# Second cross attention: a row of its own for the queries' bias in the score product

## The reference

```python
def _L1_xattn_ref(q, k, v, Wq, bq, Wk, bk, Wv, bv, Wo, bo):   # 16 heads of 8
    qh = (q @ Wq + bq).reshape(B, LQ, HEADS, D_K).transpose(0, 2, 1, 3)
    kh = (k @ Wk + bk).reshape(B, LKV, HEADS, D_K).transpose(0, 2, 1, 3)
    vh = (v @ Wv + bv).reshape(B, LKV, HEADS, D_K).transpose(0, 2, 1, 3)
    scores = jnp.einsum('bhqd,bhkd->bhqk', qh, kh) * (1.0 / np.sqrt(D_K))
    attn = jax.nn.softmax(scores, axis=-1)
    out = jnp.einsum('bhqk,bhkd->bhqd', attn, vh)
    return out.transpose(0, 2, 1, 3).reshape(B, LQ, D_MODEL) @ Wo + bo

x = _layernorm(x + _L1_xattn_ref(x, ctx_512, ctx_512, ...), axis=-1)
```

## Time and profile before

| | |
|---|---|
| median of 3 runs | 689.21 us (686.73 to 691.59) |
| profiled execution | 686.46 us |
| its span, first to last instruction | 684.7 us |
| mean granted TensorE clock | 0.999 |
| PE busy | 634.4 us (93%) |
| DVE busy | 507.3 us (74%) |
| ACT busy | 335.1 us (49%) |
| POOL busy | 348.3 us (51%) |
| chain that ended last | PE 72%, DVE 13%, ACT 9%, issue 5% |

### The profile page before, as it was taken

One profiled execution on the slowest core, in us unless ns is written; L12 is line 12 of the kernel. 1 busy time (PEld: TensorE's weight loads), 2 busy tenths in 40 slices (PEclk: granted clock), 3 DMA queues, 4 the chain that ended last, 5 costly groups with the idle time before them and its releaser, 6 DMA issues.

```text
span 684.7 us, 20022 instructions
## 1 busy us (share of the span) xinstructions
PE 634.4 (93%) x8872; PEld 474.1 (69%) x8872; DVE 507.3 (74%) x822; ACT 335.1 (49%) x502; POOL 348.3 (51%) x257
## 2 busy tenths in 40 slices
PE   8798989999999999999898889899999999998997
PEld 4576766677777777777785656677776677776774
DVE  3666837799989888885464756798888988988443
ACT  2154463555646646635325244446556365464443
POOL 1362670188888888464110422195675755745400
PEclk9999999999999999999999999999999999999999
DMA  9600003000000000000040000000000000000000
GB/s 264 231 1 2 3 1 131 2 2 2 2 2 2 3 2 2 2 2 2 2 153 0 1 1 2 1 2 2 2 2 3 2 2 2 2 2 2 2 1 14
DMA packets 3506, 14.74 MB, mean 22 GB/s; under 512 B 372, under 2 KB 628, under 8 KB 3420
## 3 DMA queue, kind: packets, MB, share of 16 engines
q1 hardware_dynamic: 3420, 13.46, 5.9%
HBM read 13.23 MB, written 0.23 MB: 20 GB/s over the span
## 4 chain that ended last, share of the span: by engine, by line
PE 72%; DVE 13%; ACT 9%; issue 5%; DMA 1%; DVEq 0%; ACTq 0%
PE psum L987 18%; PE psum L891 10%; PE psum L200 6%; PE psum L940 5%; PE psum L933 5%; PE psum L935 5%; DVE scratch L1085 2%; DVE scratch L1070 2%; PE psum L870 2%; ACT scratch L1054 2%; PE psum L897 1%; PE psum L224 1%; PE psum L879 1%; PE psum L229 1%; PE psum L909 1%
## 5 line engine op out<-in xcount | busy, mean ns | idle before, releaser
L1070 POOL TENSOR_TENSOR scratch<-scratch 125x896 bf16<-125x896 f32 x136 | 234.9, 1734 | 173.1 <-ACT scratch L1054 173.0
L1054 ACT ACTIVATE scratch<-psum 125x896 f32<-125x896 f32 x192 | 173.8, 917 | 175.6 <-PE psum L987 173.8
L1085 DVE TENSOR_REDUCE scratch<-psum 128x1 f32<-128x500 f32 x336 | 210.7, 673 | 16.6 <-PE psum L891 8.1
L987 PE MATMUL psum<-scratch 128*125 128x448 bf16 (+1 forms) x768 | 177.2, 355 | 9.1 <-issue 8.8
L891 PE MATMUL psum<-scratch 128*128 128x500 bf16 x336 | 126.0, 375 | 2.0 <-ACT nrm L1021 0.8
L987 PEld LDWEIGHTS psum<-scratch 128*125 128x125 bf16 (+1 forms) x768 | 97.3, 136 | 39.8 <-issue 9.5
L933 PE MATMUL psum<-tok,scratch 125*128 125x65 bf16 x1344 | 108.9, 195 | 1.8 <-DVE kT L1130 1.8
L935 PE MATMUL psum<-tok,scratch 125*128 125x64 bf16 x1344 | 108.3, 192 | 0.0
L933 PEld LDWEIGHTS psum<-tok,scratch 125*128 125x128 bf16 x1344 | 95.5, 97 | 13.8 <-issue 2.6
L935 PEld LDWEIGHTS psum<-tok,scratch 125*128 125x128 bf16 x1344 | 90.3, 99 | 14.4
L200 PE MATMUL psum<-w_second 128*128 128x256 bf16 x638 | 85.3, 272 | 0.0
(11 more groups left out here) (311 smaller groups left out, 814.3 us busy)
## 6 DMA issues: line engine op xcount, KB each, us to landing
raw<-ctx_dram SPq DMA_DIRECT2D x4, 672.0 KB
w_third<-fifth_dram SPq DMA_DIRECT2D x3, 636.0 KB, 5.2
w_third<-third_dram SPq DMA_DIRECT2D x2, 844.0 KB, 21.2
w_third<-third_dram SPq DMA_DIRECT2D x2, 843.5 KB, 19.4
w_fourth<-fourth_dram SPq DMA_DIRECT2D x3, 542.5 KB, 6.1
w_first<-first_dram SPq DMA_DIRECT2D x1, 996.0 KB, 5.0
w_second<-second_dram SPq DMA_DIRECT2D x1, 834.0 KB, 6.9
w_third<-fifth_dram SPq DMA_DIRECT2D x1, 636.5 KB, 7.4
```

Source lines behind the costliest of these rows:

```text
L987: mm = nc.tensor.matmul(bank(S + f, HALF, CP), lhs[0:rows, CP * c:CP * c + CP], rhs[0:rows, HALF * f:HALF * f + HALF], start=(rows == 128) ...
L1054: nc.scalar.activation(CR["p"][0:CP, n % RING, :].rearrange("p (f n) -> p f n", f=2), psum[0:CP, S:S + 2, 0:HALF], ACT.Exp).then_inc(self. ...
L1070: ops.tensor_tensor(CR["pl"][0:CP, n % RING, :], CR["p"][0:CP, n % RING, :], p_high(n % RING), ALU.subtract).then_inc(done, 1)
L1085: nc.vector.tensor_reduce(mxp[:, r, t:t + 1], bank(B, TB), X_AXIS, ALU.max).then_inc(self.aux_freed, 1)
```

## The change

The low queries `qb` get the bias row as row 96, and `yb` has ones in the rows 64 to 96, so that the product adds it to every score. The rows between, 65 to 95 of `qb`, are zero. The second product of a score has 97 rows in the second attention where it had 65. ScalarE's copy goes to partition 96 of `qb`, not to partition 64 of `qx`, which is gone. In A, VectorE subtracts the bias row from the turned maximum and writes the result to row 64, once; the semaphore `top_set` and the addition behind it are gone. The ones rows cover 33 partitions in `cross2`, and GpSimd sets rows 64 to 95 of `qb` to zero in two more memsets before `cross2`; the first M of the batches 0 and 1 and, new, VectorE's A of the same batches wait for all of them.

```diff
--- before.py
+++ after.py
@@ -148,7 +148,6 @@
             CR["ya", i] = R.take([CTX], BF16)
             CR["yb", i] = R.take([CTX], BF16)
             CR["qa", i] = R.take([896], BF16)
-            CR["qx", i] = nrm[:, 7 * i:7 * i + 7, :].rearrange("p a b -> p (a b)").bitcast(BF16)
             CR["qb", i] = R.take([896], BF16)
         CR["p"] = R.take([RING, 896])
         CR["pl"] = R.take([RING, 896], BF16)
@@ -181,10 +180,14 @@
         tok_scaled = sem("token_scaled")
         y_ones = sem("y_ones")
 
-        def y_ones_set(pool, done):
+        def y_ones_set(pool, biased):
+
             for i in range(2):
-                nc.gpsimd.memset(CR["yb", i][64:65, :], 1.0).then_inc(y_ones, 1)
-                pool.wait_ge(y_ones, done + i + 1)
+                nc.gpsimd.memset(CR["yb", i][64:97 if biased else 65, :], 1.0).then_inc(y_ones, 1)
+                pool.wait_ge(y_ones, 2 * biased + i + 1)
+            for i in range(2 * biased):
+                nc.gpsimd.memset(CR["qb", i][64:96, :], 0.0).then_inc(y_ones, 1)
+                pool.wait_ge(y_ones, 5 + i)
 
         pads_set = sem("pads_set")
         key_scaled = sem("key_weights_scaled")
@@ -798,11 +801,11 @@
             def __init__(self, tag, src, wk, wv, biased):
                 self.tag, self.src, self.wk, self.wv, self.biased = tag, src, wk, wv, biased
                 (self.aux_ready, self.aux_freed, self.scores, self.probs, self.pv_done, self.mean_turned, self.tok_high,
-                 self.tok_set, self.ya_set, self.yb_set, self.q_high, self.max_set, self.top_set, self.rec_set, self.mean_set, self.low_dve,
+                 self.tok_set, self.ya_set, self.yb_set, self.q_high, self.max_set, self.rec_set, self.mean_set, self.low_dve,
                  self.low_pool, self.front_act, self.front_dve, self.front_low) = (
                     sem(f"{tag}_{n}") for n in (
                         "aux_ready", "aux_freed", "scores", "probs", "pv", "mean_turned", "tok_high", "tok_set",
-                        "ya_set", "yb_set", "q_high", "max_set", "top_set", "rec_set", "mean_set", "low_dve", "low_pool",
+                        "ya_set", "yb_set", "q_high", "max_set", "rec_set", "mean_set", "low_dve", "low_pool",
                         "front_act", "front_dve", "front_low"))
 
                 self.order = [(u, 0) for u in FRONT]
@@ -886,7 +889,7 @@
                         else:
                             pe.wait_ge(self.front_dve, 2)
                         if b < 2:
-                            pe.wait_ge(y_ones, 2 if self is cross1 else 4)
+                            pe.wait_ge(y_ones, 6 if self.biased else 2)
                     r, t = k // TBLK, k % TBLK
                     mm = nc.tensor.matmul(bank(B, TB), CR["qa", i][:, 128 * r:128 * r + 128],
                                           CR["ya", i][:, TB * t:TB * t + TB], start=True, stop=True)
@@ -982,11 +985,12 @@
                         pe.wait_ge(self.yb_set, 2 * (b + 1))
                         pe.wait_ge(self.front_low, 2)
                     S = 2 + 2 * (n % 2)
-                    for lhs, rhs, rows in ((CR["ya", i], CR["qa", i], 128), (CR["yb", i], CR["qb", i], 65)):
+                    below = 97 if self.biased else 65
+                    for lhs, rhs, rows in ((CR["ya", i], CR["qa", i], 128), (CR["yb", i], CR["qb", i], below)):
                         for f in range(2):
                             mm = nc.tensor.matmul(bank(S + f, HALF, CP), lhs[0:rows, CP * c:CP * c + CP],
                                                   rhs[0:rows, HALF * f:HALF * f + HALF],
-                                                  start=(rows == 128), stop=(rows == 65), skip_group_check=True)
+                                                  start=(rows == 128), stop=(rows != 128), skip_group_check=True)
                     mm.then_inc(self.scores, 1)
                     if c or not b:
                         sums_of_earlier()
@@ -1018,7 +1022,7 @@
                     nc.scalar.activation(CR["qa", i][0:64, cols], bank(B, HALF, 64), ACT.Copy)
                     ins = nc.scalar.activation(CR["qa", i][64:128, cols], bank(B, HALF, 64), ACT.Copy)
                     if self.biased:
-                        ins = nc.scalar.activation(CR["qx", i][64:65, cols], psum[64:65, B, 0:HALF], ACT.Copy)
+                        ins = nc.scalar.activation(CR["qb", i][96:97, cols], psum[64:65, B, 0:HALF], ACT.Copy)
                     ins.then_inc(self.q_high, 1)
                 elif kind == "T":
                     act.wait_ge(self.aux_ready, idx + 1)
@@ -1033,10 +1037,10 @@
                 act.wait_ge(self.aux_ready, 3)
                 nc.scalar.activation(CR["qa", 0][0:64, 0:HALF], bank(4, HALF, 64), ACT.Copy).then_inc(self.front_act, 1)
                 if self.biased:
-                    nc.scalar.activation(CR["qx", 0][64:65, 0:HALF], psum[64:65, 4, 0:HALF], ACT.Copy
+                    nc.scalar.activation(CR["qb", 0][96:97, 0:HALF], psum[64:65, 4, 0:HALF], ACT.Copy
                                          ).then_inc(self.front_act, 1)
                     act.wait_ge(self.front_dve, 1)
-                    nc.scalar.activation(CR["qx", 0][64:65, HALF:2 * HALF], psum[64:65, 5, 0:HALF], ACT.Copy
+                    nc.scalar.activation(CR["qb", 0][96:97, HALF:2 * HALF], psum[64:65, 5, 0:HALF], ACT.Copy
                                          ).then_inc(self.front_act, 1)
 
             def run_act(self, act):
@@ -1092,10 +1096,10 @@
                     lo, hi = (0, 512) if k == 0 else (512, 896)
                     shift, below = CR["qb", i][64:65, lo:hi], psum[64:65, B, 0:hi - lo]
                     if self.biased:
-                        bias = CR["qx", i][64:65, lo:hi]
-                        nc.vector.tensor_tensor(shift, below, bias, ALU.subtract).then_inc(self.top_set, 1)
-                        dve.wait_ge(self.top_set, 2 * b + k + 1)
-                        nc.vector.tensor_tensor(shift, shift, bias, ALU.add).then_inc(self.aux_freed, 1)
+                        if b < 2:
+                            dve.wait_ge(y_ones, 6)
+                        nc.vector.tensor_tensor(shift, below, CR["qb", i][96:97, lo:hi], ALU.subtract
+                                                ).then_inc(self.aux_freed, 1)
                     else:
                         nc.vector.tensor_copy(shift, below).then_inc(self.aux_freed, 1)
                 elif kind == "T":
@@ -1849,7 +1853,7 @@
                 cross1.split_tokens(pool, 0, k)
             pool.wait_ge(cross1.tok_set, 2)
             pool.wait_ge(a1_act.sem, a1_act.count(f"o{PAIRS-1}"))
-            y_ones_set(pool, 0)
+            y_ones_set(pool, False)
             for k in range(2):
                 cross1.split_tokens(pool, 1, k)
             cross1.run_pool(pool)
@@ -1867,7 +1871,7 @@
             cross2.split_tokens(pool, 1, 0)
             pool.wait_ge(ln_c.sem, ln_c.count("yr"))
             pool.wait_ge(cross2.tok_set, 3)
-            y_ones_set(pool, 2)
+            y_ones_set(pool, True)
             pool.wait_ge(outer, 4)
             cross2.split_tokens(pool, 1, 1)
             cross2.run_pool(pool)
```

## The result

The changed kernel takes 679.21 us (median of 4 runs, 677.76 to 681.06), the kernel before 690.3: a ratio of 0.9849 with a 95% interval of 0.9802 to 0.9896. Timed twice more, in other sets, the ratio was 0.9853 (0.9831 to 0.9876) and 0.9849 (0.9818 to 0.9880). The forecast was 679.0. The medians differ by 11.1 us in the first set and by 10.3 and 10.4 in the other two; 10.2 was forecast.

The account below looks back on a forecast made before the run. TensorE waits for VectorE's shift row at batch boundaries of the second cross attention. Savings of 8.4 + 0.64 + 0.84 + 0.3 = 10.2 us, against the median of 689.21, gave 679.0 us, range 675.0 to 683.5.

Parts of the forecast that it names:

- What bounds the boundary: Between batches of the second cross attention, TensorE's "issue" wait before a score product is for VectorE's shift row; 8.8 us over seven.
- Five boundaries at 1.68 us: Five batch boundaries of the second cross attention: score product starts at 461.33 instead of 463.01, together 8.4 us saved.
- The sixth and seventh, 0.64 and 0.84: Last two batch boundaries of the second cross attention, without GpSimd work beside them: 0.64 and 0.84 us saved.
- The front, 0.3: Before batch 0 of the second cross attention, where filler products cover most of the wait: 0.3 us saved.
- rival 1: Only TensorE's recorded idle time before score products goes: gain 9.1 us, time 680.1; chance 12%.
- Rival 3: New shift-row subtraction is slow, its second input lying in other partitions: gain 4.7 us, time 684.5; chance 7%.
- Rival 5: Another wait of the score product ends at the same moment, so nothing moves: 688 us; chance 3%.
- Rival 2: VectorE's next subtraction, started earlier, collides with GpSimd unabsorbed: 0.58 us at five boundaries, gain 7.3, time 681.9; chance 8%.
- the twin: First cross attention, same code without the keys' bias, read for comparison: 26.0 us a batch against the second's 27.8.
- The profiled execution: Whole kernel: 10.2 us off the profiled execution's 686.46 gives 676.3; against the median, 679.0.

## Why the prediction was right

- *What bounds the boundary.* Right: "issue" in front of the score product was VectorE's shift row. Taking the operation away alone empties the wait, the layout alone leaves it, and a second subtraction brings it back.
- *Five boundaries at 1.68 us.* The distance between the small reductions of two batches fell from 27.78 to 26.12 us, 1.66 each, 8.3 against 8.4.
- *The sixth and seventh, 0.64 and 0.84.* 26.76 to 26.13 is 0.63, and from the seventh boundary's reduction to the last chunk's score products 20.41 us (624.80 to 645.21) became 19.57 (618.77 to 638.34): 0.84.
- *The front, 0.3.* Mis-sized: 0.46. I took the row's idle time where I should have taken, as at the boundaries, the distance of the products in TensorE's queue. It is the same error as rival 1, in small. Sum in the trace: 8.3 + 0.63 + 0.84 + 0.46 = 10.2, as forecast.
- *Rival 1* (only the recorded idle goes, 9.1) falls by that sum. *Rival 3* (a slow subtraction): 1.16 us for the pair, although the second input lies 32 partitions off. *Rival 5* (nothing moves) falls with the waits, which are gone. *Rival 2*: the collision came, with 1.40 us instead of the twin's 1.67, and was absorbed, though earlier than I had it: in VectorE's wait for the exponential in front of the next L1074, while the wait for the bias copy stayed at 12.4 us. (The prediction has this operation start 1.76 us earlier, at 461.18; from the twin's 1.19 us behind the start of the pair follow 461.07 and 1.87, and the changed kernel has those 1.19. Nothing hangs on it.) By the rule of the Trainium skill ("SBUF — State Buffer", § SBUF: two separate sides) that two SBUF inputs contend with GpSimd's reads, these runs agree on both sides of it: L1098 and L1074 shorten when GpSimd's work is lightened, and the subtraction with one input in PSUM is 689 and 545 ns with or without it.
- *The profiled execution,* 676.3 forecast, was 679.63. The difference of 3.3 us lies in stages that the change does not touch: about 2.2 us where the clock fell, the rest in the spread in front of the first attention. It would have been better to say that before's profiled execution had a clock of 0.999 and that others might not.
- *Luck in the number.* That the median came within 0.2 us of 679.0 is partly chance. The forecast was taken from a median of 689.21; with a fourth run it was 690.3, and the measured difference in that set is 11.1 us. What is borne out is the 10.2 us: by the traces, and by the 10.3 and 10.4 of the other two sets.

## What to carry to other kernels

Where two stages share their code and differ in one operation, read one as the forecast of the other: the distance between the same two instructions in both gives the gain more exactly than the recorded idle time, whose ends are modelled. A wait of TensorE named "issue" is worth a look at what ends 0.1 us before it on the other engines. And before a wait is moved off one engine, ask whose next PSUM bank the moved operation still reads.

## What the runs showed that I had not expected

The granted clock fell in one execution and not in another of the same kernel, at places that come back: in three profiled executions of the changed kernel at 24, 338 and 403 us, at 21, 400 and 666 us, and at 22 us alone (the last few us of the program left out). In the windows shown it averaged 0.90 to 0.94, which is part of the stretch at the lower of its two levels (1.2 and 2.4 GHz). At the first place TensorE had just stood still for 2.19 us (1.95 before, where the clock stayed, and 1.68 in a later run of the changed kernel, where it fell, so the length of this wait does not decide it). In front of the second it had waited 0.42 and 0.50 us, in the execution where the clock fell and in one where it stayed. The fall at the first place was made up for within the same stage; the two later ones cost 2.2 us here, a fifth of the gain that was to be measured. Together with 1.3 us of spread at the start they explain why one pair of profiled executions, 6.9 us apart, says less than their stages do.
